# A two-layer transformer kernel on one core: the second layer's routing and its experts' weights moved into the first layer's expert loop

## The chip, the core and the metric

The kernel is one program on one core of a Trainium2 chip. The metric is the device time of one execution in microseconds (us), lower is better. TensorE (PE in the rows) multiplies matrices, VectorE (DVE) and ScalarE (ACT) work on tiles, GpSimd (POOL) does elementwise work and issues indirect DMAs, SyncE (SP) issues most other DMAs. Each engine runs its own instruction list in order; semaphores tie them together.

## The reference

1,024 tokens of 256 features go through two layers, each of a mixing part and a mixture of experts, all in float32:

```python
# layer 0
x = x + ga * attention(ln(x) * (1 + ca) + sa)            # 16 heads, causal
h = ln(x) * (1 + cb) + sb
x = x + gb * (shared_expert(h) + 64 small experts, top 6 of 64 by sigmoid, capacity 128)
# layer 1
h = ln(x) * (1 + ca) + sa
state_t = state_{t-1} * A + B h_t;  y = C state + h * D   # a scan over all tokens
x = x + ga * (ln(h + y) * w + b)
h = ln(x) * (1 + cb) + sb
x = x + gb * (8 experts of hidden size 512, top 2 of 8 by softmax, weights renormalised)
```

## The kernel before

**First expert layer (units).** It is computed densely: two halves of 512 tokens, each 17 hidden tiles (the shared expert and 16 tiles of four experts). So there are 34 units (`UNITS`), numbered u = 0 to 33; 0 to 16 are the first half's, 17 to 33 the second half's. A unit is `up(u)` on TensorE (two products of 12 matmuls), `gate_half` and `gated_high` on ScalarE, `gate(u)` and `gated_low(u)` on VectorE, and `down(u)` on TensorE, which accumulates in the bank pair `SUMS[h]`, (0,1) or (6,7). TensorE's list is `up(u)`, extras of unit u, `down(u - 2)`. Every float32 product is three matmuls of a high and a low part; SyncE loads each unit's weights (`load_weights`, seven buffers `w_raw`), GpSimd scales and splits them (`scale_down`, `weights_low`). The routing weights of a unit are a row block of `combine`, spread over partitions by `load_combine` into one of four buffers `wbc`; `gate` waits for it.

**Second layer's first half in the units.** When the first half's sums are complete (unit 16), its layer 1 work is threaded through units 18 to 33 by `if u == ...` lines on all engines: layer statistics, `both_rows(xn_h, 0, 0)` (eight transposes), `state_in` (matmuls), `scan` (DVE), `state_out`, `transpose_state`, `state_stats`, `state_weighted`, `state_added`, statistics again, `normalise_rows(4)` and `store_rows(0)` on ScalarE, `both_rows(xn_r, 0, 0)` at unit 32 and `router` at unit 33.

**Between the layers.** After the units VectorE does `route(0)` (softmax and top 2), TensorE counts pairs (`count_pairs(0)`, small matmuls with ones), VectorE makes eight full blocks of 128 pairs from the first half's tokens (`early_blocks`, `pair_places`, `pair_map`, `owners`), TensorE maps slots to tokens (`map_slots(0)`) and `slots(0)` writes the token indices. GpSimd then gathers the tokens' rows (`gather`). Beside this the second half's statistics run (`layer_out_stats(1)`; its root steps are interleaved with `early_blocks` by `input_norm`), ScalarE copies (`keep_rows(1)`) and normalises, TensorE transposes (`both_rows(xn_h, 0, 1)`), and `state_in(1)`, `map_weights(0)`, `state_out(1)` follow.

**Second expert layer (blocks).** 25 blocks b = 0 to 24 (`NB1`): 8 early ones (`NBE`) of the first half's tokens, 17 late ones. TensorE's list for a block is gate half of `half_up(b)`, `hidden(b-1)` (four transposes), `tokens(b+1)` (two transposes), value half of `half_up(b)`, `down1(b-1)`. The second half's remaining state work, its routing (`router`, `count_pairs(1)`, `map_slots(1)`, `map_weights(1)`) and its VectorE chain (`late_blocks` to `slots(1)`) are threaded through blocks 0 to 8. GpSimd's list is gather and scatter: block b's result is added to the sums in DRAM by `scatter(b)`; the gathers of late blocks are issued after `scatter(FIRST_LATE)`:

```python
            for b in range(NB1):
                scatter(b)
                if b == FIRST_LATE:
                    pool.wait_ge(slots_ready, 2)
                    pool.wait_ge(rows_stored, 32)
                    for c in range(NBE, b + NXG):
                        gather(c)
```

**Weights of the 8 experts.** `wgu` (1 MB for each expert) lies in SBUF over the first layer's unit buffers. One load is issued at unit 28, seven between the end of unit 30's `down` and the last one. TensorE waits for all 16 loads (`wgu` and `wdn`) ahead of block 0.

Of the kernel before, what the change touches and what calls it, by code (L numbers as in the profile page):

```python
# [13 lines left out]
P = 128  # L14
# [15 lines left out]
FIRST_LATE = 4  # L30
MAP_AT = (128, 256)
WEIGHTS_AT = (320, 352)
TOKENS1, HIDDEN1, DOWN1, ROUTE1, GATE1, VALUE1 = 0, 1, 2, 3, 4, 5
# [153 lines left out]
def program(nc, x_d, w_attn_d, w_out_d, qk_scale_d, gate0_d, ffn0_d, c_d, wmod_d, const_d,  # L187
# [9 lines left out]
    with ctx:  # L197
# [47 lines left out]
        sq = weights("sq", [P, HPG * HD])  # L245
        sqk = weights("sqk", [P, HD])
        (const,) = stage(("const", [P, 4 * P + 1], F32))
        qT_hi, qT_lo = [], []
        for c in range(2):
            qT_hi.append(weights(f"qT_hi{c}", [P, HPG, 512], F32R))  # L250
            qT_lo.append(weights(f"qT_lo{c}", [P, HPG, 512], F32R))
# [5 lines left out]
        weights("under_wo", [P, HPG, D])  # L257
        (v_hi, v_lo, prob, pT_hi, pT_lo, oT_hi, oT_lo, r_sb, o_f, mx, negb, rsum, rinv, rqs, gabs) = stage(
# [29 lines left out]
        w_sp, wbc, fa, _, _, _, fc, hid_hi, hid_lo = stage(  # L288
            ("w_sp", [P, NW, 2, 6 * P], F32R), ("wbc", [P, NC0, 512], F32), ("fa", [P, 2, 512], F32),
            ("beside_expert", [P, 2 * 256], F32), ("last_expert", [P, 8 * 256], F32), ("beside_fa", [P, 2, 512], F32),  # L290
            ("fc", [P, 2, 512], F32), ("hid_hi", [P, 2, 512], F32R), ("hid_lo", [P, 2, 512], F32R))
        (w_raw,) = stage(("w_raw", [P, NW, 2, 6 * P], F32))
        (wgu, chosen, placed, at_pair, fill, fill_key, picked, fill_top, taken,
         ends, count_i, pos_i, in_block, block_at, block_end, owner, code, token_f, empty, token_i, pair_i, owner_i,
         wpair, wslot, spare_row, fa1, hid1, slot_hot, block_hot, block_eq,
         pw_top, pw_rest, block_w) = stage(
            ("wgu", [P, E1, KC * 2 * H1], F32),
# [9 lines left out]
            ("slot_hot", [P, PAIRS, SLOTS1], BF16), ("block_hot", [P, PAIRS, 2 * NBL], BF16),  # L307
            ("block_eq", [P, PAIRS, NBL], F32), ("pw_top", [P, NT, TOPK1], BF16), ("pw_rest", [P, 2, NT, TOPK1], F32),
            ("block_w", [P, PAIRS, 3, NBL], BF16))
        keep("under_layers", [P, 88 * 256])  # L310
# [5 lines left out]
        hs = keep("hs", [P, T])  # L316
        zT = keep("zT", [P, KC, 512])
# [5 lines left out]
        x_b = keep("x_b", [P, NT, D])  # L323
        wmod1 = [wmod1_t[:, kc, :] for kc in range(KC)]
# [32 lines left out]
        yo_out = [sem(f"yo_out{b}") for b in range(NYO)]  # L357
        x_final, x_in_sums, weights_spread, weights_mapped = [sem(n) for n in (
# [17 lines left out]
        norm_step = sem("norm_step")  # L376
# [29 lines left out]
        def _(sp):  # L406
# [21 lines left out]
            def load_gate_up(e):  # L428
                sp.dma_start(wgu[:, e, :], gate_up_d[:, e, :]).then_inc(w1_loaded, 16)
# [26 lines left out]
            for u in range(1, 4):  # L456
                load_combine(u)
# [39 lines left out]
        def _(pool):  # L497
# [81 lines left out]
            for u in range(3, UNITS):  # L579
                weights_low(u)  # L580
                if u + 2 < UNITS:
                    scale_down(u + 2)
                if u == 25:
                    shifted_rows(0)
# [41 lines left out]
        def _(act):  # L626
# [200 lines left out]

            for u in range(UNITS):
# [25 lines left out]
                if u == 20:  # L854
                    act.wait_ge(x_kept, 2)
                    normalise_rows(3, tiles_of(0))
                if u == 22:
# [3 lines left out]
                if u == 31:  # L861
                    normalise_rows(4, tiles_of(0), last=True)
                if u == 32:
                    store_rows(0, 16)
                    act.wait_ge(z_ready, 2)
                    for kc in range(KC):
                        modulate(3, 1, 4, kc, SUMS[0] + kc)
                gated_high(u)
# [1289 lines left out]
```

## Time and profile before

| | |
|---|---|
| device time, three runs | 861.97, 862.66, 857.64 us (median 861.97) |
| profiled execution, its own device time | 857.57 us |
| its span, first to last instruction | 855.7 us |
| TensorE busy | 788.4 us (92%) |
| VectorE, ScalarE, GpSimd busy | 539.8, 459.6, 259.2 us |
| mean granted TensorE clock | 0.979 of full speed |
| units 18 to 33 with their last downs | about 594 to 672.3 us of the span |
| last down to block 0's first matmul | 672.3 to 691.5 us |
| blocks | 691.5 to 843.7 us, out copy 849.6 us |

Stages are given in us from the span's start. The last column pair of a windows row is DMA activity; the number ahead of it is the granted TensorE clock (1.00 is 2.4 GHz, 0.50 is 1.2 GHz).

### The profile page before, as it was taken

To read this page: it belongs to the slowest core of one execution; us is meant where nothing else is said; L and a number is where in the kernel's file an instruction comes from. 1 tells how busy PE (TensorE), PEld (TensorE's weight loads), DVE (VectorE), ACT (ScalarE), POOL (GpSimd) and SP (SyncE) were. 2 spreads that over 40 slices of the span, in tenths; PEclk is the share of its full clock that TensorE was granted. 3 is DMA by queue.
4 is the path that set the end of the run, shared out by engine and by line. 5 is a ranking of instruction groups with operands and counts; after the bars stand their busy time and mean duration, and the time that the engine had idled before them with its cause. 6 is when DMAs were issued, how large, how long until landed. Compare 5 with 4: busy or idle time off the path is not lost.

```text
span 855.7 us, 13741 instructions
## 1 busy us (share of the span) xinstructions
PE 788.4 (92%) x4674; PEld 642.5 (75%) x4674; DVE 539.8 (63%) x1321; ACT 459.6 (54%) x993; POOL 259.2 (30%) x185
## 2 busy tenths in 40 slices
PE   6887999989999989999899989999998589999994
PEld 5765888877788877888778778888887546666662
DVE  6567768677668667586786865685687776411211
ACT  3555766757648567467584825755544334233230
POOL 1004301017010061010150124666663033444432
PEclk9898999999999999999999999999999899999997
DMA  7010000010000100000010005565665822332322
GB/s 270 1 38 1 1 1 1 1 62 2 1 2 2 38 26 1 1 1 1 26 59 1 20 31 176 178 193 168 186 198 172 336 81 57 55 50 39 49 31 67
DMA packets 23459, 56.14 MB, mean 66 GB/s; under 512 B 2736, under 2 KB 10032, under 8 KB 22224
## 3 DMA queue, kind: packets, MB, share of 16 engines
q1 hardware_dynamic: 15792, 45.83, 16.2%
q0 software_dynamic: 4800, 6.56, 4.8%
q10 hardware_dynamic: 2800, 2.88, 1.0%
q8 instruction: 39, 0.64, 0.3%
q14 instruction: 28, 0.23, 0.1%
HBM read 48.97 MB, written 7.34 MB: 66 GB/s over the span
## 4 chain that ended last, share of the span: by engine, by line
PE 75%; DVE 11%; DMA 6%; ACT 3%; issue 3%; SPq 0%; POOLq 0%; DVEq 0%; ACTq 0%
PE ps L1632 16%; PE ps L1633 15%; PE ps L1634 15%; PE ps L2027 10%; PE ps L1737 6%; PE ps L2045 5%; DMA wbc<-combine 4%; DVE mx L1066 2%; DVE pT_lo L1080 1%; PE ps L1879 1%; PE ps L2037 1%; PE ps L1866 1%; DMA combine<-wT 1%; DMA wqkv_raw<-in_w_attn 1%; DVE o_f L1168 1%
## 5 line engine op out<-in xcount | busy, mean ns | idle before, releaser
L735 ACT ACTIVATE prob<-ps,negb,rqs 128x128 f32<-128x128 f32 (+7 forms) x128 | 106.7, 834 | 70.4 <-DVE negb L1071 69.0
L513 POOL TENSOR_TENSOR oT_lo<-o_f,oT_hi 128x512 fp32r<-128x512 f32 x32 | 41.6, 1300 | 301.4 <-ACT oT_hi L814 301.4
L724 ACT ACTIVATE pT_hi<-ps 128x512 fp32r<-128x512 f32 (+1 forms) x192 | 88.8, 491 | 63.3 <-PE ps L1737 57.7
L1066 DVE TENSOR_REDUCE mx<-ps 128x1 f32<-128x128 f32 (+7 forms) x128 | 96.5, 754 | 25.1 <-PE ps L1729 24.1
L1080 DVE TENSOR_TENSOR pT_lo<-ps,pT_hi 128x512 fp32r<-128x512 f32 (+1 forms) x192 | 99.9, 548 | 2.5 <-ACT pT_hi L724 2.4
L2027 PE MATMUL ps<-wgu,xgT 128*128 x200 | 94.2, 594 | 1.0 <-ACT xgT L888 1.0
L1737 PE MATMUL ps<-ident,prob 128*128 128x128 f32 x576 | 86.4, 276 | 0.9 <-DVE qT_lo L1102 0.6
L1632 PE MATMUL ps<-pT_hi,v_hi 128*128 128x512 f32 x192 | 73.6, 383 | 12.7 <-DVE pT_lo L1080 12.7
L1632 PE MATMUL ps<-kT_hi,qT_hi 128*128 128x512 f32 (+1 forms) x192 | 70.3, 366 | 5.6 <-ACT prob L735 3.9
L539 POOL TENSOR_TENSOR w_sp<-w_raw,w_sp 128x768 fp32r<-128x768 f32 x34 | 64.8, 1905 | 33.1 <-ACT w_sp L709 33.1
L1634 PE MATMUL ps<-kT_hi,qT_lo 128*128 128x512 f32 (+1 forms) x192 | 66.9, 348 | 0.0
L1633 PE MATMUL ps<-kT_lo,qT_hi 128*128 128x512 f32 (+1 forms) x192 | 66.8, 348 | 0.0
L1634 PE MATMUL ps<-pT_hi,v_lo 128*128 128x512 f32 x192 | 66.8, 348 | 0.0
L1633 PE MATMUL ps<-pT_lo,v_hi 128*128 128x512 f32 x192 | 66.6, 347 | 0.0
L602 POOL DMA_INDIRECT sums<-yo,pair_i x25 | 39.5, 1582 | 88.7 <-DVE yo L1571 72.0
L905 ACT ACTIVATE fa<-ps 128x512 f32<-128x512 f32 x25 | 14.9, 598 | 92.8 <-PE ps L2027 92.8
L1737 PEld LDWEIGHTS ps<-ident,prob 128*128 128x128 f32 x576 | 61.9, 142 | 2.9 <-DVE v_lo L1089 0.9
L1564 DVE TENSOR_TENSOR hid<-fa,ps 128x512 f32<-128x512 f32 x25 | 17.2, 687 | 70.9 <-PE ps L2027 65.3
L826 ACT ACTIVATE hid_hi<-fc 128x512 fp32r<-128x512 f32 x34 | 21.4, 631 | 65.3 <-DVE fc L1250 54.7
L2027 PEld LDWEIGHTS ps<-wgu,xgT 128*128 128x128 f32 x200 | 35.8, 190 | 26.7 <-issue 25.6
L1632 PE MATMUL ps<-hT_hi,w_sp 128*128 128x512 f32 x136 | 54.8, 403 | 0.3 <-issue 0.3
L1634 PE MATMUL ps<-hT_hi,w_sp 128*128 128x512 f32 x136 | 54.3, 400 | 0.0
(296 smaller groups left out, 2051.1 us busy)
## 6 DMA issues: line engine op xcount, KB each, us to landing
w_raw<-in_ffn SPq DMA_DIRECT2D x34, 384.0 KB, 6.8
wbc<-combine SPq DMA_DIRECT2D x32, 256.0 KB
wgu<-in_gate_up SPq DMA_DIRECT2D x8, 1024.0 KB, 8.9
wdn<-in_down SPq DMA_DIRECT2D x8, 512.0 KB, 10.2
wqkv_raw<-in_w_attn SPq DMA_DIRECT2D x4, 768.0 KB, 4.3
wo_raw<-in_w_out SPq DMA_DIRECT2D x4, 512.0 KB, 3.3
wmod_t<-in_wmod SPq DMA_DIRECT2D x1, 1536.0 KB, 13.9
x<-in_x ACTq DMA_DIRECT2D x2, 512.0 KB, 6.9
```

The costliest lines, as they stand in the source:

```text
L513: nc.gpsimd.tensor_tensor(oT_lo[:, m % HPG, :], o_f[:], oT_hi[:, m % HPG, :], ALU.subtract).then_inc(oT_lo_done, 1)
L539: nc.gpsimd.tensor_tensor(w_sp[:, b, 1, :], w_raw[:, b, 1, :], w_sp[:, b, 0, :], ALU.subtract).then_inc(w_ready, 1)
L724: nc.scalar.activation(pT_hi[:, unit % NUNITS, 0:nb, qi * P:(qi + 1) * P], ps[:, ROTATING[place % 3], 0:nb * P].rearrange("p (j t) -> p j ...
L735: nc.scalar.activation(prob[:, n % 3, 0:w], ps[:, pair:pair + 2, :].rearrange("p b k -> p (b k)")[:, 0:w], ACT.Exp, bias=negb[:, n % 2:n % ...
L1066: nc.vector.reduce_max(mx[:, i:i + 1], ps[:, pair:pair + 2, :].rearrange("p b k -> p (b k)")[:, 0:w], AX.X).then_inc(row_max, 1)
L1080: nc.vector.tensor_tensor(pT_lo[dst], ps[:, ROTATING[place % 3], 0:nb * P].rearrange("p (j t) -> p j t", j=nb), pT_hi[dst], ALU.subtract). ...
L1632: nc.tensor.matmul(out, w_hi_, m_hi, start=start, stop=False, skip_group_check=True)
L1633: nc.tensor.matmul(out, w_hi_, m_lo, start=False, stop=False, skip_group_check=True)
L1634: return nc.tensor.matmul(out, w_lo_, m_hi, start=False, stop=stop, skip_group_check=True)
L1737: ins = nc.tensor.transpose(ps[:, ROTATING[place % 3], j * P:(j + 1) * P], prob[:, k % 3, (j0 + j) * P:(j0 + j + 1) * P], ident[:])
L2027: ins = nc.tensor.matmul(ps[:, bank, :], xgT[:, b % 2, kc, :], wgu[:, bass.ds(e, 1), c:c + H1].rearrange("p a c -> p (a c)"), start=(kc == ...
L2045: ins = nc.tensor.matmul(ps[:, DOWN1, 0:D], hidT[:, b % 2, c, :], wdn[:, bass.ds(e, 1), c, :].rearrange("p a d -> p (a d)"), start=(c == 0 ...
```

## The change

It moves work between the three stages and reorders it.

- The first half's layer 1 chain runs two to four units earlier (statistics wholly at unit 18, transposes and modulate at 20, `state_in` 21, `state_out` 22, `transpose_state` 23, VectorE's steps packed in units 21 to 26, last transposes at 28, `router` at 29).
- `both_rows(…)` and `count_pairs(0)` in the units stand behind `down(u - 2)` instead of ahead of it.
- `route(0)`, the new `pair_weights(0)`, `early_blocks`, `pair_places`, `owners`, `pair_map` and `slots(0)` run in units 29 to 33; `count_pairs(0)` and `map_slots(0)` on TensorE in units 30 and 33. `chances(0)` (an Exp on ScalarE) is at unit 29.
- Banks: the routing of the two halves gets a bank each (1 and 3), so `count_pairs(1)` counts all eight tiles, not four.
- `load_combine` is issued one unit sooner. Weights of experts 0 and 1 are loaded at units 8 and 11, those of 3, 4, 5, 2, 6 as unit buffers come free, and expert 7's after the last `down`, under a semaphore of its own that TensorE waits for at block 4. SBUF tiles change places for this.
- Behind the last `down` TensorE does only `tokens(0)` and `both_rows(xn_h, 0, 1)` before block 0. `state_in(1)` and `map_weights(0)` come behind block 0's gate half, `state_out(1)` behind its value half, `transpose_state(1)` in block 1.
- In the blocks, `both_rows(xn_r, 4, 1)` and `router` move from block 3 to 4, `count_pairs(1)` from 4 to 5, `map_slots(1)` from 6 to 7, the VectorE chain to `slots(1)` with them by one block, and `FIRST_LATE` from 4 to 5.

```diff
-FIRST_LATE = 4
+FIRST_LATE = 5
+ROUTE1 = (1, 3)
...
-                if u % (1 + IT0):
-                    load_combine(u)
+                if u + 1 < UNITS and (u + 1) % (1 + IT0):
+                    load_combine(u + 1)
...
-                if u == 28:
-                    load_gate_up(7)
-
-            for e in range(3):
-                sp.wait_ge(down_done, UNITS - 4 + e)
-                load_gate_up(e)
+                if u in (8, 11):
+                    load_gate_up((u - 8) // 3)
+
+            sp.wait_ge(down_done, 29)
+            load_gate_up(3)
+            sp.wait_ge(down_done, 31)
+            load_gate_up(4)
+            sp.wait_ge(down_done, 32)
+            load_gate_up(5)
             sp.wait_ge(weighted, UNITS)
-            load_gate_up(5)
+            load_gate_up(2)
+            sp.wait_ge(down_done, 33)
             load_gate_up(6)
             sp.wait_ge(down_done, UNITS)
-            load_gate_up(3)
-            load_gate_up(4)
+            load_gate_up(7, w1_last)
...
# VectorE, in the loop over units
                 if u == 18:
                     layer_out_stats(0)
-                if u == 19:
                     variances(tiles_of(0))
                     root_steps(tiles_of(0))
                     shifts(tiles_of(0))
...
+                if u == 24:
+                    variances(tiles_of(0))
+                    root_steps(tiles_of(0))
+                    state_weighted(0)
+                if u == 25:
+                    state_added(0)
+                    link(stats(xt, tiles_of(0)))
                 if u == 26:
                     variances(tiles_of(0))
                     root_steps(tiles_of(0))
+                    shifts(tiles_of(0))
+                if u == 29:
+                    route_shift(0, SUMS[0])
+                    route(0)
+                if u == 30:
+                    pair_weights(0)
+                    early_blocks()
+                if u == 31:
+                    pair_places(HT)
+                    owners(NBE, 0)
+                if u == 32:
+                    pair_map(HT, NBE)
                 if u == UNITS - 1:
-                    route_shift(0, SUMS[0])
+                    slots(0, NBE, 0)
...
# TensorE, in the loop over units
+                if u == 29:
+                    pe.wait_ge(h_full, 12)
+                    router(wgate1, E1, SUMS[0], 0)
+                if u == UNITS - 1:
+                    map_slots(0, HT, NBE)
+                if u >= 2:
+                    down(u - 2)
+                if u == 30:
+                    count_pairs(0)
+                if u == 28:
+                    pe.wait_ge(rows_normed, 16)
+                    both_rows(xn_r, 0, 0)
+                if u == 20:
                     pe.wait_ge(rows_normed, 12)
                     pe.wait_ge(x_kept, 2)
                     both_rows(xn_h, 0, 0)
...
# TensorE, blocks
+            tokens(0)
+            pe.wait_ge(rows_normed, 18)
+            pe.wait_ge(ln_normed, NT + 2)
+            pe.wait_ge(x_kept, 4)
+            both_rows(xn_h, 0, 1)
             pe.wait_ge(owners_ready, 1)
-            pe.wait_ge(w1_loaded, 16 * 2 * E1)
-            tokens(0)
+            pe.wait_ge(w1_loaded, 16 * (2 * E1 - 1))
...
+                    if b == NBE - TB1:
+                        pe.wait_ge(w1_last, 16)
-                    if b == 6:
+                    if b == 7:
                         map_slots(1, NT, NBL)
-                    if b == 8:
-                        map_weights(1, NT, NBL)
                     half_up(b, e, 0, GATE1, gate_done)
                 if b == 0:
-                    transpose_state(1)
+                    state_in(1)
+                    map_weights(0, HT, NBE)
                 if b > 0:
                     hidden(b - 1)
                 if b + 1 < NB1:
                     tokens(b + 1)
...
+                if b == 0:
+                    state_out(1)
+                if b == 8:
+                    map_weights(1, NT, NBL)
```

## Rows read from the trace of the kernel before

**Rows 1.** Windows by stage: span; busy us (count) of PE, PEld, DVE, ACT, POOL; clock; DMA share; GB/s.
```profile
594.00:672.30 78.30, 74.94 (x434) 63.91 (x432) 54.10 (x118) 36.81 (x60) 37.65 (x27) 1.00 0.63 199
672.30:691.50 19.20, 8.48 (x49) 4.61 (x48) 16.39 (x87) 4.65 (x9) 5.89 (x5) 0.73 0.75 281
691.50:840.60 149.10, 149.09 (x637) 94.53 (x638) 52.73 (x161) 49.92 (x105) 57.63 (x45) 1.00 0.28 48
```
**Rows 2.** Waits of PE, 594 to 672.5 us: total us, times, longest.
```profile
PE ps L1646 <- ACT xn_r L677: 2.7, 1, 2.7
PE ps L1632 <- DVE hid_lo L1255: 0.6, 1, 0.6
```
**Rows 3.** Timeline of SP, two consecutive units: start us, us.
```profile
638.23 0.33 SPq L426 DMA_DIRECT2D w_raw<-in_ffn  x1
642.45 0.32 SPq L426 DMA_DIRECT2D w_raw<-in_ffn  x1
```
**Rows 4.** Timeline of PE between the layers: start us, us.
```profile
672.04 0.28 PE L1634 MATMUL ps<-w_sp,hid_lo 128*128 128x256 f32 x1
...
680.02 1.97 PE L1646 MATMUL ps<-ident,xn_h 128*128 128x128 f32 x8 [5.48 <-ACT xn_h L677]
...
691.51 1.98 PE L2027 MATMUL ps<-wgu,xgT 128*128 x4 [0.98 <-ACT xgT L888]
```
**Rows 5.** Timelines of DVE and ACT: the second half's statistics.
```profile
674.50 1.42 DVE L955 BATCH_NORM_STATS2 stat<-ps 128x6 f32<-128x256 f32 x4
...
678.88 1.09 ACT L677 ACTIVATE xn_h<-x,shift,rs_y 128x256 f32<-128x256 f32 x2 [1.84 <-DVE shift L975]
```
**Rows 6.** Critical chain, variances to shift of the first half: start us, us.
```profile
654.60 0.29 DVE mv L960 x4
656.70 1.72 DVE shift L975
```
**Rows 7.** Critical chain: moved TensorE groups where they run at full clock.
```profile
615.59 1.72 PE ps L1907 x4
...
741.34 0.42 PE ps L2001 x16
```
**Rows 8.** Windows of 2 us between the layers, columns as in group 1.
```profile
674.00:676.00 2.00, 0.51 (x14) 0.41 (x14) 1.86 (x8) 0.04 (x1) 0.00 (x0) 1.00 1.00 414
676.00:678.00 2.00, 0.00 (x0) 0.00 (x0) 1.97 (x19) 1.04 (x2) 0.00 (x0) 0.52 0.99 418
686.00:688.00 2.00, 1.11 (x10) 0.27 (x8) 1.66 (x5) 0.00 (x0) 1.42 (x2) 0.92 0.30 84
```
**Rows 9.** The tile wgu: time from issue to landing of its eight loads.
```profile
DMA to landing us min/median/max: 4.7/8.9/12.0
```
**Rows 10.** Timelines of PE, DVE and POOL, blocks 6 and 7.
```profile
729.05 0.56 PE L1991 MATMUL ps<-block_hot,slot_hot 128*128 128x34 bf16 x16
731.69 0.38 PE L2020 MATMUL ps<-ident,xg 128*128 128x128 f32 x2
...
737.51 0.38 PE L2020 MATMUL ps<-ident,xg 128*128 128x128 f32 x2
...
730.51 0.18 DVE L1529 TENSOR_SCALAR token_i<-token_f 128x17 int32<-128x17 int32 x1
...
730.25 1.55 POOL L602 DMA_INDIRECT sums<-yo,pair_i  x1 [3.54 <-DVE yo L1571]
732.11 1.01 POOL L589 DMA_INDIRECT xg<-rows,token_i  x1 [0.30 <-issue]
```
**Rows 11.** The tile xg: gathers over the whole kernel, then those of 680 to 700 us.
```profile
DMA to landing us min/median/max: 2.6/2.8/5.4
...
DMA to landing us min/median/max: 2.6/2.7/3.1
```
**Rows 12.** Timeline of DVE: unit 18's combine row arrives; a vector step of a unit.
```profile
595.43 0.69 DVE L1250 TENSOR_TENSOR fc<-ps,wbc 128x512 f32<-128x512 f32 x1 [2.32 <-DMA wbc<-combine]
...
646.74 0.69 DVE L1247 TENSOR_TENSOR ps<-fa,ps 128x512 f32<-128x512 f32 x1
```

More of the change, by code:

```diff
@@ L455, in _ @@
                 load_weights(u)
-            for u in range(1, 4):
+            for u in range(1, 5):
                 load_combine(u)
@@ L897, in hidden_in @@
                                      ACT.Copy).then_inc(hidT_ready, 1)
+            act.wait_ge(logits_done, 3)
             tokens_in(0)
+            for kc in range(KC):
+                modulate(4, 1, 0, kc, SUMS[1] + kc)
             for b in range(NB1 + 1):
@@ L1929, in both_rows, with count_pairs, map_slots, map_weights @@
                     transpose_rows(rows, t0, kc, SUMS[h] + kc)
+            def count_pairs(h):
+                pe.wait_ge(chosen_ready, h + 1)
+                bank = ROUTE1[h]
+                last = 4 * h + 3
+                for t in range(last + 1):
+                    for q in range(t + 1):
+                        nc.tensor.matmul(ps[:, bank, t * E1:(t + 1) * E1], (before_b if q == t else ones_b)[:],
+                                         sel_b[:, q, 0:E1], start=(q == 0), stop=(q == t), skip_group_check=True)
+                for q in range(last + 1):
+                    ins = nc.tensor.matmul(ps[:, bank, (NT + h) * E1:(NT + h + 1) * E1], ones_b[:], sel_b[:, q, 0:E1],
+                                           start=(q == 0), stop=(q == last), skip_group_check=True)
+                ins.then_inc(counted1, 1)
+            def map_slots(i, nt, nb):
+                pe.wait_ge(map_ready, i + 1)
+                hits = ps[:, ROUTE1[i], MAP_AT[i]:MAP_AT[i] + 2 * nb].rearrange("p (a n) -> p a n", a=2)
+                np_ = TOPK1 * nt
+                for j in range(np_):
+                    ins = nc.tensor.matmul(hits, slot_hot[:, j, :],
+                                           block_hot[:, j, :].rearrange("p (a n) -> p a n", a=2)[:, :, 0:nb],
+                                           start=(j == 0),
+                                           stop=(j == np_ - 1), skip_group_check=True)
+                ins.then_inc(mapped, 1)
+            def map_weights(i, nt, nb):
+                pe.wait_ge(weights_spread, i + 1)
+                sums = ps[:, ROUTE1[i], WEIGHTS_AT[i]:WEIGHTS_AT[i] + 3 * nb].rearrange("p (a n) -> p a n", a=3)
+                for j in range(TOPK1 * nt):
+                    ins = nc.tensor.matmul(sums, slot_hot[:, j, :], block_w[:, j, :, 0:nb], start=(j == 0),
+                                           stop=(j == TOPK1 * nt - 1), skip_group_check=True)
+                ins.then_inc(weights_mapped, 1)
             for u in range(UNITS + 2):
@@ L1974, in count_pairs @@
-            def count_pairs(h):
-                pe.wait_ge(chosen_ready, h + 1)
-                for t in tiles_of(h):
-                    for q in range(t + 1):
-                        nc.tensor.matmul(ps[:, ROUTE1, t * E1:(t + 1) * E1], (before_b if q == t else ones_b)[:],
-                                         sel_b[:, q, 0:E1], start=(q == 0), stop=(q == t), skip_group_check=True)
-                last = 4 * h + 3
-                for q in range(last + 1):
-                    ins = nc.tensor.matmul(ps[:, ROUTE1, (NT + h) * E1:(NT + h + 1) * E1], ones_b[:], sel_b[:, q, 0:E1],
-                                           start=(q == 0), stop=(q == last), skip_group_check=True)
-                ins.then_inc(counted1, 1)
@@ L1997, in map_weights @@
-            def map_weights(i, nt, nb):
-                pe.wait_ge(weights_spread, i + 1)
-                sums = ps[:, ROUTE1, WEIGHTS_AT[i]:WEIGHTS_AT[i] + 3 * nb].rearrange("p (a n) -> p a n", a=3)
-                for j in range(TOPK1 * nt):
-                    ins = nc.tensor.matmul(sums, slot_hot[:, j, :], block_w[:, j, :, 0:nb], start=(j == 0),
-                                           stop=(j == TOPK1 * nt - 1), skip_group_check=True)
-                ins.then_inc(weights_mapped, 1)
@@ L2005, in _ @@
-            count_pairs(0)
-            pe.wait_ge(rows_normed, 18)
-            pe.wait_ge(ln_normed, NT + 2)
-            pe.wait_ge(x_kept, 4)
-            both_rows(xn_h, 0, 1)
-            map_slots(0, HT, NBE)
-            state_in(1)
-            map_weights(0, HT, NBE)
-            state_out(1)
             def tokens(b):
```

337 lines of the change are left out of this document (141 added, 196 removed).

## The prediction, as it was put on record

> **What bounds the kernel now.** I read the windows by stage first, then TensorE's waits and timeline, then the chain. TensorE is busy for 149.09 of the 149.10 us of the blocks and for 74.94 of 78.30 us of units 19 to 33 [rows 1]: both loops run at the pace of TensorE. A unit takes 4.22 us, the distance of two loads that a finished `down` releases [rows 3]. Idle TensorE time in that stage is 2.7 us before the transposes at unit 32, which wait for ScalarE's rows, and 0.6 us before a `down` that waits for VectorE [rows 2]; the restarts behind them and slack between groups are about 1.0 us more, by the count of units and groups in the stage. Between the layers, from the last `down`'s end at 672.3 to block 0's first matmul at 691.5, TensorE is busy for 8.48 of 19.2 us while VectorE is busy for 16.39 [rows 1, 4]: the routing chain stands there, at a clock that falls to one half [rows 8]. So what can be won lies in 4.3 us of the units and 19.2 us between the layers; the blocks can only get longer.
>
> **The units.** Moved in: `count_pairs(0)` and `map_slots(0)`, 14 and 8 matmuls of a few columns; the 16 of `map_slots(1)` take 0.56 us [rows 10], so 0.5 and 0.4 us: +0.9 us. The other groups only change place within the stage. Gone if all is in time: the 4.3 us. What is late next is VectorE. A unit costs it three steps of 0.69 us [rows 12], 2.1 of 4.22 us; a low part may come some 8.4 us behind its `up` before TensorE waits, since two units of TensorE's work lie between. Unit 18 gets 1.42 us of statistics [rows 5] and the 2.1 us from variances to shift, which can be drawn out by up to 1.6 us (the shift itself took 1.72 us, where each of the ten steps takes about 0.2 [rows 6]). Carried forward from the combine row that lands at 595.4 [rows 12], unchanged since it waits for the same store: shift at 600 to 601.4, ScalarE's four rows (twice the 1.09 us of two [rows 5]) by 602.1 to 603.6, while TensorE wants them at 602.5 for the transposes at unit 20. A stall of 1.0 us. `load_combine` one unit sooner takes away VectorE's waits for rows, which TensorE felt only as the 0.6 us; at unit 17 it puts unit 21's weights behind a combine load that waits for its store, and what GpSimd then is late I count within the same 1.0. Unit 24 adds 3.7 us, unit 25 3.1, unit 26 2.1; carried forward in the same way, unit 26's low part and ScalarE's rows come 0 to 1.3 us late at unit 28: 0.5 us. Routing in units 29 to 32 adds some 10 to 14 linked steps each, at 0.2 us a step 2 to 3 us against the 2.1 free in a unit; the slack takes it up. In unit 33 `slots(0)`, seven steps, stands ahead of the low part: `down(33)` waits 0.8 us. Sum: -4.3 + 0.9 + 1.0 + 0.5 + 0.8 = -1.1, I take -1.0; the ends are -3.4 (no stall) and +2 (each chain drawn out once more). Experts 0 and 1 at units 8 and 11 add 2 MB where TensorE's weights are loaded units ahead: nothing, and if that cover were gone, one load's 2.6 us. The two table loads around `chances(0)` fall in ScalarE, busy for under half of the stage [rows 1]: nothing.
>
> **Between the layers.** What stays behind the last `down`: statistics 1.42, variances to shift 2.1, then ScalarE's two rows 1.09 [rows 5, 6], with semaphores 5.0 us; then eight transposes, 1.97 us as now at half clock [rows 4]. Together 7.0 against 19.2 us: -12.2. The tokens of block 0 are gathered from about 668.6 on and land in 2.6 to 5.4 us [rows 11], before the transposes. In these rows the six first gathers took 2.6 to 3.1 us [rows 11] though weights were still coming in at the start. The Trainium skill, DMA: Bandwidth & Descriptors, Queues, rings and completion order, says that a DMA engine goes round its queues packet by packet; by that rule the gather passes the weights' queue, and were it not so it would land some 8 us later and the gain of this stage would shrink by about 5 us. The trace agrees as far as it goes, but has no gather in the middle of 4 MB.
>
> **Weights.** Expert 5, 2 and 6 are released at about 667.5 to 669 and are 3 MB. At the 414 to 418 GB/s of [rows 8] that is 7.5 us, 676 to 677 with start and end; the transposes end near 678.3. Covered by 1.3 us. The loads took 4.7 to 12.0 us each in such a queue [rows 9]; at the upper end the wait would cost 3 us.
>
> **Work moved into the blocks.** `state_in(1)`, `state_out(1)` and `map_weights(0)` leave a stretch where TensorE was idle anyway and stand now where it is the bound: 1.72 us each for the two groups of four matmuls of 512 columns and 0.42 us, at full clock [rows 7], and ten more small matmuls in `count_pairs(1)`, 0.3 us: +4.1. The clock: before, TensorE stopped at 672.3, was at half by 676 and back at full about 6.3 us after the transposes began at 680.0 [rows 4, 8]. Now it stops for 5 us, so I expect the fall again, and the return some 6 us after the transposes start: block 0's gate half, as many columns as `state_in(1)`, at 1.2 GHz: twice 1.72 in place of 1.98 us [rows 4, 7], and 0.45 us of `state_in(1)`: +1.9. It could be 0 (no fall; the transposes would then be 1.0 us cheaper too). `down1(2)` waits about 0.3 us for `expert_out(1)`, which now stands behind the statistics of the new rows.
>
> **The late gathers.** Everything up to `slots(1)` moves one block back, but block 8's tokens are still wanted in block 7. Before: mapping at 729.05, indices at 730.69, scatter of block 4 from 730.25, first late gather at 732.11, landing 2.8 us later at about 734.9, and `tokens(8)` not before 737.51: 2.6 us in hand [rows 10, 11]. Now `tokens(8)` stands where `tokens(7)` stood, 2.6 us behind the mapping (731.69), and the rows land 5.9 us behind it: TensorE waits 3.2 us. On its queue behind that wait stand the value half and `down1(6)`. A block has nothing to hide it: +3.2, between 2.5 and 5.8 by the landing times of [rows 11].
>
> **Sum.** -1.0 - 12.2 + 4.1 + 1.9 + 0.3 + 3.2 = -3.7 us. The profiled execution took 857.57 us (855.7 us of span and 1.9 around it), so it would be 853.9. It lies at the foot of the three runs, 4.4 us under their median; on the median's footing I say 858. About 1% (8.6 us) is what a measurement here can tell from no change.
>
> **Rivals.**
> 1. More is won. The clock does not fall (-1.9 and -1.0) or the late gather is covered (-3.2), or both: -6.6, -6.9 or -9.8, so 848 to 851 on the profile's footing and 852 to 855 on the median's. For: the pause is 5 us against 7.7 before, and clock windows need not fall alike. Against: it had fallen after 3.7 us, and the gather's order is fixed in the list. Chance 0.30, both together 0.18.
> 2. The weights or the first tokens arrive late, since 4 MB, the gathers and the sums' store share the engines in 12 us: up to 3 to 5 us more, so -0.7 to +1.3, 861 to 863 on the median's footing. For: 1.3 us of cover only. Chance 0.15.
> 3. On the other side: VectorE becomes the bound of units 24 to 33. Its list holds about 25 linked small steps of routing ahead of `gated_low`, and each chain can be drawn out by 1.6 us as the shift was [rows 6]. Five chains drawn out give 8 us, 1.5 of them inside the slack; TensorE then waits before `down(29)` to `down(33)`: +6.5, so +2.8 over now, 865 on the median's footing. It decides when more than three chains are drawn out. For: GpSimd's splits run through unit 30. Against: VectorE is busy for 54.1 of 78.3 us [rows 1], and GpSimd stops there. Chance 0.10; about half of it or less passes +1%.
> 4. The change does not shorten the gap, because the second half's own chain was as long as the routing: out, its parts are 5.0 us [rows 5, 6]. Chance under 0.02.
>
> My forecast has 0.45. The range has to take in rival 1 and most of 2 and 3, and that the medians of three scatter by 5 us: 849 to 865. Faster by over 1% comes from rival 1 with both parts, and a little from a gap or a unit stage that is better than I think: 0.22. Slower by over 1% comes from rival 3 and its like: 0.08. Within 1%: 0.70.
>
> **What would show it.** The windows: last `down`'s end near 671.3, block 0's first matmul 7 us later, its duration 3.4 us (clock at half) or 1.7. TensorE's waits: about 3 us before the transposes of xg at block 7, and about 1 us before `both_rows` at unit 20. Blocks 1 to 24 otherwise at the same pace. I am wrong if the gap is over 10 us, if block 7 shows no wait, or if TensorE waits more than 4 us in the units.

## The result, and the profile after

| | before | after |
|---|---|---|
| device time, median of four runs | 862.03 us (857.64 to 862.66) | 877.12 us (876.91 to 877.19) |
| profiled execution: device time, span | 857.57, 855.7 us | 877.19, 875.4 us |
| mean granted TensorE clock | 0.979 | 0.971 |

After to before 1.0193, 95% interval 1.0162 to 1.0225: slower, by some 2%. I had forecast 858.0 us, 849 to 865. The profiled execution of before is as fast as the fastest of its four, so the two profiled ones lie 19.6 us apart where the medians lie 15.1.

I cut the span at three marks that every run here has: the start of `both_rows(xn_h, 0, 1)` at unit 5, the end of the last `down`, and block 0's first matmul. Up to the first mark the kernels are alike but for the first units.

| profiled execution, us | to unit 5 | unit 5 to last `down` | gap | block 0 to end | span |
|---|---|---|---|---|---|
| before | 533.2 | 139.1 | 19.2 | 164.2 | 855.7 |
| after | 535.5 | 153.6 | 9.9 | 176.4 | 875.4 |

"Gap" is the time between the last `down` and block 0. It did get shorter by 9.3 us and the blocks longer by 12.2; both have the predicted sign. The units, where I had a gain of 1.0, lost 14.5.

TensorE's waits of the changed kernel, units 5 to 29 (engine, tile, line, releaser: total us, times, longest):

```profile
PE ps L1618 <- POOL w_sp L546: 8.1, 8, 1.9
PE ps L1618 <- DVE hid_lo L1261: 1.2, 1, 1.2
PE ps L1754 <- ACT hT_h L662: 0.4, 1, 0.4
```

Up to the end of the units 1.3 us for `slot_hot` and 0.6 for a low part of `hid` are added, at unit 33. In [rows 2] no line on `w_sp` stands: TensorE now waits in `up` for GpSimd's low part of the weights, seven of the eight times between 563 and 616 us. One step back, GpSimd's timeline of the changed kernel, around the first of these stalls:

```profile
560.77 0.74 POOL L540 TENSOR_TENSOR w_raw<-w_raw,gates 128x256 f32<-128x256 f32 x1 [3.90 <-DMA w_raw<-in_ffn]
561.47 1.80 POOL L546 TENSOR_TENSOR w_sp<-w_raw,w_sp 128x768 fp32r<-128x768 f32 x1
565.72 0.89 POOL L540 TENSOR_TENSOR w_raw<-w_raw,gates 128x256 f32<-128x256 f32 x1 [2.45 <-DMA w_raw<-in_ffn]
```

GpSimd is early too; it waits for the load of `w_raw`. The chain of waits of the changed kernel names these loads (start us, us, what):

```profile
526.00 9.29 DMA w_raw<-in_ffn
...
552.95 12.70 DMA w_raw<-in_ffn
...
572.96 14.65 DMA w_raw<-in_ffn
...
601.62 11.04 DMA w_raw<-in_ffn
```

A load of 384 KB under way for 15 us: in the whole kernel they take 2.9, 8.5 and 14.8 us (least, median, most), where they took 2.9, 6.8 and 9.6. So look at the DMA engines, in windows where combine loads alone are moving: the first two of these three (the third is for the clock). The changed kernel (columns as in [rows 1]):

```profile
560.00:563.00 3.00, 1.40 (x12) 1.20 (x11) 1.18 (x2) 0.84 (x1) 2.23 (x2) 1.00 0.26 102
576.00:580.00 4.00, 3.07 (x42) 2.54 (x40) 2.84 (x3) 1.55 (x3) 2.29 (x2) 1.00 0.26 98
617.00:619.00 2.00, 2.00 (x6) 1.62 (x5) 0.82 (x1) 0.92 (x2) 2.00 (x2) 0.50 0.55 154
```

TensorE stands still for half of the first window, and the sixteen DMA engines are busy for 0.26 at 98 to 102 GB/s, where they can do 414 [rows 8]. The kernel before has the same figure, at the end of its units:

```profile
650.00:655.00 5.00, 5.00 (x33) 4.47 (x32) 4.37 (x13) 2.22 (x4) 2.68 (x3) 1.00 0.26 99
```

0.26 is, within a hundredth, four engines of sixteen. The load's source is four rows, each read 32 times, and four is the outermost dimension of its pattern. The Trainium skill, DMA: Bandwidth & Descriptors, in the section on why a DMA increments its semaphore by 16, has the rule: the number of engines is the largest one up to 16 that divides the slowest dimension that is not 1 of both patterns. The share agrees.

That gives the sum that I hadn't made. For each unit, one of the four engines moves 64 KB of a combine load, 24 KB of `w_raw` (384 KB over 16) and 10.7 KB of `wdn` (512 KB every third unit): 98.7 KB. At the rows' 25 KB/us (100 GB/s over four) this is, as an estimate, 3.9 of a unit's 4.22 us. Each early expert load adds 64 KB, 2.6 us, and 0.3 us is free in a unit: by this estimate two such loads three units apart make a queue that lasts to the end of the half (unit 17 needs no combine row). SyncE's list shows the same from the other side. I take it that an issue lasts longer when its queue has no room. SyncE, changed kernel:

```profile
557.59 2.00 SPq L445 DMA_DIRECT2D wbc<-combine  x1
559.63 3.29 SPq L433 DMA_DIRECT2D wgu<-in_gate_up  x1
562.97 0.59 SPq L430 DMA_DIRECT2D w_raw<-in_ffn  x1
563.66 0.57 SPq L445 DMA_DIRECT2D wbc<-combine  x1
564.27 3.65 SPq L474 DMA_DIRECT2D wdn<-in_down  x1
```

An issue of `w_raw` took some 0.33 us in [rows 3], those of `wgu` and `wdn` 0.33 to 0.49 us in the whole kernel before. The third window above shows a second price: TensorE had waited 1.8 us up to 615.7, and then ran at half clock until after 619.

TensorE in the gap, changed kernel, against [rows 4]:

```profile
692.67 0.69 PE L2001 MATMUL ps<-ident,xg 128*128 128x128 f32 x2 [3.60 <-DMA xg<-first_rows,token_i]
694.17 1.97 PE L1632 MATMUL ps<-ident,xn_h 128*128 128x128 f32 x8 [0.81 <-ACT xn_h L684]
699.00 3.78 PE L2008 MATMUL ps<-wgu,xgT 128*128 x4 [2.86 <-issue]
702.57 3.20 PE L1893 MATMUL ps<-hT_h,bT 128*128 128x512 f32 x4
```

and at block 7, against [rows 10]:

```profile
755.69 0.44 PE L2001 MATMUL ps<-ident,xg 128*128 128x128 f32 x2 [3.11 <-DMA xg<-rows,token_i]
755.96 3.17 PE L2008 MATMUL ps<-wgu,xgT 128*128 x4
758.92 2.34 PE L2026 MATMUL ps<-wdn,hidT 128*128 x8
```

The late gather costs 3.11 us where I had 3.2; that the clock then falls I had not counted. Four matmuls take 3.17 us there, and the next groups of the kind 1.88.

### The profile page after: what moved, and what is told of

Same layout as the page of the kernel before. It is cut to its first block, busy times and chain, and to the rows that moved or that the text cites. A ratio compares the mean times of both kernels' runs of the same rounds, so it can differ in the third digit from the quotient of the medians.

```text
span 875.4 us, 13755 instructions
## 1 busy us (share of the span) xinstructions
PE 801.0 (92%) x4684; PEld 649.3 (74%) x4684; DVE 544.4 (62%) x1321; ACT 461.3 (53%) x993; POOL 260.3 (30%) x185
## 4 chain that ended last, share of the span: by engine, by line
PE 70%; DVE 11%; DMA 9%; issue 4%; ACT 3%; POOL 1%; SPq 1%; POOLq 0%; DVEq 0%; ACTq 0%
PE ps L1618 14%; PE ps L1619 13%; PE ps L1620 13%; PE ps L2008 9%; PE ps L1723 6%; DMA w_raw<-in_ffn 5%; PE ps L2026 4%; DVE mx L1072 2%; DVE pT_lo L1086 1%; PE ps L1865 1%; DMA wgu<-in_gate_up 1%; PE ps L2018 1%; PE ps L1852 1%; PE ps L1641 1%; POOL w_sp L546 1%
## 5 line engine op out<-in xcount | busy, mean ns | idle before, releaser
L2008 PE MATMUL ps<-wgu,xgT 128*128 x200 | 97.4, 610 | 2.9 <-issue 2.9
L1618 PE MATMUL ps<-hT_hi,w_sp 128*128 128x512 f32 x136 | 57.0, 419 | 8.2 <-POOL w_sp L546 8.1
L2008 PEld LDWEIGHTS ps<-wgu,xgT 128*128 128x128 f32 x200 | 36.6, 194 | 29.6 <-issue 28.5
L1620 PE MATMUL ps<-hT_hi,w_sp 128*128 128x512 f32 x136 | 55.3, 407 | 0.0
L1619 PE MATMUL ps<-hT_lo,w_sp 128*128 128x512 f32 x136 | 55.1, 405 | 0.0
```

The costliest lines, as they stand in the source:

```text
L1618: nc.tensor.matmul(out, w_hi_, m_hi, start=start, stop=False, skip_group_check=True)
L1619: nc.tensor.matmul(out, w_hi_, m_lo, start=False, stop=False, skip_group_check=True)
L1620: return nc.tensor.matmul(out, w_lo_, m_hi, start=False, stop=stop, skip_group_check=True)
L2008: ins = nc.tensor.matmul(ps[:, bank, :], xgT[:, b % 2, kc, :], wgu[:, bass.ds(e, 1), c:c + H1].rearrange("p a c -> p (a c)"), start=(kc == ...
```

## The experiments

Theories: **A**, the combine loads keep four DMA engines nearly full and 2 MB more overflow them; **B**, the new place of `load_combine` in SyncE's list is the cause; **C**, VectorE's load is. Times are medians; the run of before on the same chips stood at 860.7 to 861.5.

**1. The order of the combine loads undone.**

```diff
-            for u in range(1, 5):
+            for u in range(1, 4):
                 load_combine(u)
...
-                if u + 1 < UNITS and (u + 1) % (1 + IT0):
-                    load_combine(u + 1)
+                if u % (1 + IT0):
+                    load_combine(u)
```

> Of the changed kernel one part is undone: load_combine is issued in its old order again (units 1 to 3 ahead of the loop, load_combine(u) instead of load_combine(u + 1) in it). Theory A (the two early expert loads are what is late: combine loads keep four of the sixteen DMA engines nearly full, at a DMA share of 0.25 to 0.27, and 2 MB more overflow them): GpSimd's waits for w_raw stay near 55 us, TensorE's waits for w_sp stay at 6 to 8 us, the time stays within 1.5 us of the changed kernel's. Theory B (the order is the cause: unit 17 puts unit 21's weights behind a combine load that waits for its store, and the combine load stands ahead of the weights' load): GpSimd's waits fall back to about 26 us, TensorE's waits for w_sp disappear, the kernel is 6 to 9 us faster than the changed one.

874.6 us (1.016 of before, 1.013 to 1.019), 2.5 us under the changed kernel: more than A's 1.5, far from B's 6 to 9. In the profiled executions the stages from unit 5 on gained nothing (340.3 us against 339.9; units 152.2 against 153.6). Some details speak for B: the waits for `w_sp` are gone but for 0.3 us, and GpSimd's for `w_raw`, from 520 to 675 us, fell from 45.2 to 33.1 us (26.1 before). But in their place TensorE waits for VectorE (from 520 us on), and VectorE for combine rows, 29.4 us where the changed kernel has 19.1:

```profile
PE ps L1618 <- DVE hid_lo L1261: 8.5, 7, 3.7
```

I read it so: weights and combine rows share the four engines, and the order only decides which of them is late. B is out as the cause of the lost time, and my expectation that the waits would stay where they were was wrong.

**2. Experts 0 and 1 loaded late.**

```diff
-                if u in (8, 11):
-                    load_gate_up((u - 8) // 3)
+                if u in (25, 28):
+                    load_gate_up((25, 28).index(u))
```

> Of the changed kernel the loads of experts 0 and 1 are issued at units 25 and 28 instead of 8 and 11. Theory A (2 MB overflow the four engines that the combine loads use): the stalls behind w_raw between units 11 and 24 disappear, 6.1 us of waits for w_sp between 560 and 610 among them, and come back in part behind unit 25, where ten units of queue are left, so 2 to 5 us of waits there; time 2 to 5 us under the changed kernel. Theory B (order of the combine load): the stalls stay where they are, between 560 and 616, and the time stays or rises by the 2 us of the later loads.

868.0 us (1.0087, 1.0062 to 1.0112), 9 us under the changed kernel where I had expected 2 to 5. Of 8.1 us of waits for `w_sp`, 0.4 stay. Units 145.1 us. The 2 MB at units 8 and 11 account for 8.5 of the 14.5 us that the units lost.

**3. Combine loads in four.**

```diff
-                sp.dma_start(wbc[:, k % NC0, :], rows0[i - 1][:, 512 * h:512 * h + 512].unsqueeze(1).to_broadcast(
-                    [EPT0, H0, 512])).then_inc(wbc_in[k % NC0], 16)
+                for j in range(EPT0):
+                    sp.dma_start(wbc[H0 * j:H0 * j + H0, k % NC0, :],
+                                 rows0[i - 1][j:j + 1, 512 * h:512 * h + 512].to_broadcast([H0, 512])
+                                 ).then_inc(wbc_in[k % NC0], 16)
```

VectorE waits for 64 in place of 16.

> Of the changed kernel each combine load is issued as four, one for each of the four expert rows, 32 partitions of 2 KB each. Theory A (the load's outermost dimension of 4 puts it on four of sixteen engines): each part is spread over all engines, the share in stretches that hold only combine loads rises from 0.25 to 0.27 toward 1 and they land sooner; GpSimd's waits for w_raw fall under 26 us, TensorE's waits for w_sp go, and with them the clock's fall at 617: 7 to 10 us faster than the changed kernel, about 868 to 870. Theory B (order): unit 17's weights are still blocked behind the wait for the store, 1.8 us of the waits and the fall of the clock near 616 stay, and the rest changes by under 2 us. Theory C (VectorE's load is the cause): no change beyond 1 us.

864.2 us (1.0039, 1.0021 to 1.0058): 13 us under the changed kernel, more than the 7 to 10 expected, with every load of it where it was. In the profiled executions 11.1 us of it lie behind the start of unit 5. In the one microsecond behind four such issues (587 to 588 us) the DMA share is 0.48, not the 1 that I had expected, but above 0.26. Time to landing of `w_raw` and SyncE's issues in this run:

```profile
DMA to landing us min/median/max: 2.9/3.9/6.8
```

```profile
588.20 1.76 SPq L446 DMA_DIRECT2D wbc<-combine  x4
590.00 0.42 SPq L476 DMA_DIRECT2D wdn<-in_down  x1
```

Waits for `w_sp` 0.3 us; From 520 us on VectorE waits 1.6 us for combine rows, where it waited 19.1 after the change and 29.6 before it. A holds; C does not explain the loss, for VectorE's work is the same here.

**4. Tokens of block 8 behind the value half.**

```diff
-FIRST_LATE = 5
+FIRST_LATE = 4
...
-                if b + 1 < NB1:
+                if b + 1 < NB1 and b + 1 != NBE:
                     tokens(b + 1)
...
                     half_up(b, e, 1, VALUE1, value_done)
+                if b + 1 == NBE:
+                    tokens(NBE)
```

> Of the changed kernel two lines: FIRST_LATE is 4 again, so the late gathers stand ahead of the scatter of block 5, and tokens(8) stands behind the value half of block 7 instead of ahead of it. By the prediction's step for the late gathers (TensorE waits 3.1 us with the value half queued behind it, and the clock falls behind the stop, about 1.7 us more in two groups at half clock): the wait shrinks from 3.1 to 0 to 0.5 us, the clock stays at 1.00 from 755 on, 3.5 to 4.8 us less than the changed kernel. Rival: the wait moves on to the gate half of block 8, which wants ScalarE's copy of the same rows, and only the scatter's 1.1 us are won.

871.3 us (1.0113, 1.0087 to 1.0140), 5.8 less; block 0 to end 171.1 us against 176.4. TensorE, at the same place:

```profile
752.89 0.44 PE L2001 MATMUL ps<-ident,xg 128*128 128x128 f32 x2 [0.23 <-DMA xg<-rows,token_i]
753.16 1.92 PE L2026 MATMUL ps<-wdn,hidT 128*128 x8
754.92 1.88 PE L2008 MATMUL ps<-wgu,xgT 128*128 x4
```

A 3.1 us stop in the blocks costs 5.3 us with the clock behind it, a little more than the 3.5 to 4.8 expected.

**5. The kernel before, combine loads in four.** Edit 3 on the kernel before.

> The kernel before with one edit: each combine load is issued as four, one for each expert row. Its TensorE waits for nothing that these loads hold up except 0.6 us for a low part and half a microsecond of the start of unit 18. Theory A (four engines nearly full, but not over in the kernel before): within 1.5 us of before, though VectorE's waits for wbc, 29.6 us now, shrink to under 15 and w_raw lands in 4 us at the median in place of 6.8. If instead the kernel before was already held up by these engines in a way that I don't see, it gains more than 3 us.

858.0 us (0.9959, 0.9939 to 0.9978): 2.8 us faster, between my two cases (from unit 5 on 321.3 us against 322.5 in the profiled executions). The 2.7 us wait for ScalarE's rows at unit 32 [rows 2] is gone with VectorE's waits for combine rows (29.6 to 2.2 us), so a good part of what the change set out to win in the units was this load too. Units 135.3 us, 3.8 less; the gap takes 2.3 back, at half clock until 690.

**6. The kernel before, combine loads in two.**

```diff
+                for j in range(0, EPT0, 2):
+                    sp.dma_start(wbc[H0 * j:H0 * j + 2 * H0, k % NC0, :],
+                                 rows0[i - 1][j:j + 2, 512 * h:512 * h + 512].unsqueeze(1).to_broadcast([2, H0, 512])
+                                 ).then_inc(wbc_in[k % NC0], 16)
```

> The kernel before with each combine load issued as two loads of two expert rows each (outermost dimension 2). If the outermost dimension sets how many DMA engines a load uses, each part runs on two engines: 256 KB then take 5.3 us or more in each unit of 4.2 us (2.67 us on four engines, twice that on two), the DMA share in stretches with combine loads alone is 0.13, TensorE waits for VectorE or GpSimd in most units, and the kernel is over 25 us slower than before. If the limit of 0.26 is the number of loads under way or the size of one load instead, two loads are as fast as one or faster and the time stays within 2 us.

935.3 us (1.0872, 1.0824 to 1.0921). Windows of this run with combine loads alone:

```profile
537.00:538.00 1.00, 1.00 (x10) 1.00 (x10) 0.00 (x0) 0.89 (x2) 0.86 (x1) 1.00 0.13 46
...
564.00:565.00 1.00, 1.00 (x10) 1.00 (x10) 0.00 (x0) 0.00 (x0) 0.85 (x1) 1.00 0.13 49
```

0.13 is two engines. If both halves of a load use the same two, 128 + 24 + 10.7 KB at 25 KB/us make 6.5 us for a unit; if they used different ones, each engine would have no more to move than before. From unit 5 to the last `down` it took 207.8 us, 68.7 more than before over 27 combine rows, so about 2.5 us more a unit: 6.7. That fits the same two. This is the rule's strongest test here, since the bytes and the work are the same.

**7. Both edits, 3 and 4.**

> The changed kernel with both edits, combine loads in four and the two lines for the late gathers (FIRST_LATE 4, tokens(8) behind the value half). The two stalls lie 80 us apart on different queues, so the gains add: 864.2 less the 5.8 us that the second edit gave alone, 858.4 us; if part of the 5.8 us was scatter between runs, 858.4 to 860.5. What stays against the prediction is then the gap between the layers at 10 us in place of 7 and 3 us of waits in the last units.

861.0 us (1.0009, 0.9990 to 1.0028), 0.5 us above the upper end of what I expected: as fast as before. To run 3 the second edit adds 3.2 us in the medians and 4.0 in the stages from unit 5 on, not 5.8: the blocks get 4.7 us shorter, the gap 0.7 longer.

**8. Expert 6 waited for at block 4.**

```diff
-            load_gate_up(6)
+            load_gate_up(6, w1_last)
...
-            pe.wait_ge(w1_loaded, 16 * (2 * E1 - 1))
+            pe.wait_ge(w1_loaded, 16 * (2 * E1 - 2))
...
-                        pe.wait_ge(w1_last, 16)
+                        pe.wait_ge(w1_last, 32)
```

> As the kernel with both edits, and expert 6's weights come under the later semaphore, so that TensorE waits for them at block 4 and not ahead of block 0 (for these inputs no earlier block has that expert). If the last 2.9 us ahead of block 0 are the weights (the chain runs through a load of 10.4 us that lands 1.1 us before the first matmul), one load of 1 MB less at 400 to 414 GB/s is 2.5 us: the gap is 7.5 us in place of 10.1, the kernel 2.5 us faster than the one with both edits. If it is GpSimd's gather or the clock that holds block 0, under 0.5 us.

856.1 us (0.9949, 0.9930 to 0.9969), 4.9 less than run 7, where 2.5 was expected. The gap is 6.9 us, the 7.0 of the prediction, so 3.7 of the 4.9 are there. The chain of run 3 (combine loads in four) shows what had stood there:

```profile
673.26 10.36 DMA wgu<-in_gate_up
683.62 1.15 issue
684.77 3.78 PE ps L2010 x4
```

"Issue" is here a wait for weights. The version rests on these inputs, in which no block before 4 has expert 6, and isn't one to keep.

**9. `map_slots(0)` behind `down(31)`,** by moving its two lines under those of `down(u - 2)`.

> The kernel with both edits (combine loads in four, tokens(8) behind the value half), and map_slots(0) stands behind down(31) instead of ahead of it. If its 2.2 us wait for slot_hot and the half clock behind it are what the last units cost beside the plan: down(31) covers 1.4 us of the wait, but slots(0) stands ahead of the low part of unit 33 on VectorE and now waits for the later mapping, so down(33) can come up to 2 us late: 0 to 2 us less than 861.0 us. If the clock's fall is what counts and it stays away: 2 to 3.5 us less.

857.4 us (0.9955, 0.9933 to 0.9977), 3.6 less than run 7 and, by the medians, faster than before; from unit 5 on the profiled executions show 1.6 us less than run 7, and 323.3 us against before's 322.5. The units are no shorter (143.5 us): 2.2 us of waits for `slot_hot` became 0.5, and those for low parts of `hid` rose from 2.1 to 3.1 us. There was no half clock to win back either: in run 7 it stands at 1.00 from 668 to 672 us, behind the same wait. The gap is what is shorter, 8.2 us against 10.6. The last load that block 0 waits for is issued at 672.10 and lands 10.35 us later, in run 7 at 672.41 and 11.61 us later. Why, I can't show; `down(31)`, which releases expert 5's load, no longer waits for the map.

**10. And `slots(0)` behind the low part of unit 33, `tokens(0)` behind `both_rows(xn_h, 0, 1)`.**

> As the one with map_slots(0) behind down(31), and slots(0) stands behind the low part of unit 33 on VectorE, and tokens(0) behind both_rows(xn_h, 0, 1) on TensorE. The wait for slot_hot and the half clock go from the last units (3 to 3.5 us), and the tokens come later, but block 0 still waits for its weights, which are released by the last downs: 3 us less than 861.0, so 858. If the weights are bound by DMA bandwidth from their release on, the last unit ends earlier but the releases too, so that the gap stays near 10 us. Rival: the gathers, now issued some 3 us later in the middle of the weights, land up to 8.2 us after their issue and hold block 0: no gain.

858.7 us (0.9964, 0.9939 to 0.9990), near the 858 expected, but not for the reason I gave. Units 143.1, gap 8.6: no better than run 9. TensorE's waits, 665 to 700 us:

```profile
PE ps L1634 <- ACT xn_h L686: 5.1, 1, 5.1
PE ps L1620 <- DVE hid_lo L1263: 1.3, 2, 1.0
PE ps L2010 <- ACT xgT L895: 1.0, 1, 1.0
```

Neither the gathers nor the weights are last here: the second half's own chain is, then the transposes, `tokens(0)` and ScalarE's copy in series.

**11. And expert 6 at block 4.**

> As the one before, and expert 6's weights are waited for at block 4. That edit gave 4.9 us to the kernel with both edits (861.0 to 856.1). If weights and last units are separate terms, 3 us more than that: 853. If the gathers become what is late, 856 or more and a wait of TensorE for xg of over 3 us ahead of block 0.

856.5 us (0.9952, 0.9929 to 0.9975), where I had 853: with weights no longer last, the series of run 10 sets the end (TensorE's three waits are the same), and the edit of run 8 is worth some 2 us, within the two intervals, and not 4.9.

**12. GpSimd's pass in two halves.**

```diff
-                nc.gpsimd.tensor_tensor(w_sp[:, b, 1, :], w_raw[:, b, 1, :], w_sp[:, b, 0, :],
+                nc.gpsimd.tensor_tensor(w_sp[:, b, 1, 0:3 * P], w_raw[:, b, 1, 0:3 * P], w_sp[:, b, 0, 0:3 * P],
+                                        ALU.subtract)
+                nc.gpsimd.tensor_tensor(w_sp[:, b, 1, 3 * P:], w_raw[:, b, 1, 3 * P:], w_sp[:, b, 0, 3 * P:],
                                         ALU.subtract).then_inc(w_ready, 1)
```

> The kernel with both edits, and GpSimd's pass over a unit's weights (1.82 us) is cut into two passes of half the columns, about 0.93 us each. In all ten cases so far a small VectorE step that took 1.3 to 1.8 us instead of 0.2 began less than 0.6 us behind the start of such a pass and ended with it. If the step is held until GpSimd's instruction ends, the longest small VectorE step in units 18 to 33 is now 1.0 us or less, the shift at unit 26 among them, and TensorE's wait for the low part behind it falls from 1.25 to about 0.4 us: 0.5 to 1.5 us less than 861.0. If the steps are drawn out for another reason (a semaphore, a queue), they stay at 1.7 us.

860.7 us (0.9987, 0.9967 to 1.0007): no measurable gain, but the mechanism is as expected. VectorE's shift in unit 26 without the edit (the run with combine loads in four), and GpSimd beside it:

```profile
638.75 1.70 DVE L983 SCALAR_TENSOR_TENSOR shift<-mv,rs_y 128x4 f32<-128x4 f32 x1
```

```profile
638.60 1.83 POOL L548 TENSOR_TENSOR w_sp<-w_raw,w_sp 128x768 fp32r<-128x768 f32 x1 [2.69 <-ACT w_sp L718]
```

and with it:

```profile
642.31 0.88 DVE L985 SCALAR_TENSOR_TENSOR shift<-mv,rs_y 128x4 f32<-128x4 f32 x1
...
682.00 2.35 DVE L1460 TENSOR_TENSOR pw_rest<-wpair,pw_top 128x8 f32<-128x8 f32 x1
```

```profile
642.16 1.02 POOL L548 TENSOR_TENSOR w_sp<-w_raw,w_sp 128x384 fp32r<-128x384 f32 x1 [2.70 <-ACT w_sp L720]
```

Both times the step ends with GpSimd's pass. The last step is beside GpSimd's `x_b` pass of 2.35 us, which was not cut, and keeps its length. The longest wait for a low part of `hid` fell to 0.6 us, from 1.2 in run 7.

Stages of the profiled executions, us:

| | median | to unit 5 | units | gap | blocks to end |
|---|---|---|---|---|---|
| 1 order back | 874.6 | 532.7 | 152.2 | 11.3 | 176.8 |
| 2 experts at 25, 28 | 868.0 | 533.2 | 145.1 | 10.0 | 176.0 |
| 3 in four | 864.2 | 531.9 | 143.0 | 9.9 | 175.9 |
| 4 tokens(8) | 871.3 | 535.6 | 152.2 | 10.7 | 171.1 |
| 5 before, in four | 858.0 | 534.3 | 135.3 | 21.5 | 164.5 |
| 7 both edits | 861.0 | 531.6 | 143.0 | 10.6 | 171.2 |
| 8 and expert 6 | 856.1 | 535.3 | 143.9 | 6.9 | 170.0 |
| 9 map behind down | 857.4 | 531.9 | 143.5 | 8.2 | 171.6 |
| 10 and slots, tokens | 858.7 | 535.0 | 143.1 | 8.6 | 171.4 |
| 11 and expert 6 | 856.5 | 531.4 | 142.2 | 8.5 | 170.8 |
| 12 halves | 860.7 | 535.0 | 142.4 | 10.1 | 170.4 |

The first column shows 4 us of scatter that no edit explains: it is in the stage all kernels share. Each row is one execution, so for differences of 2 to 4 us between runs the other columns belong beside the medians.

## Why the prediction was wrong

**The step that failed** is "Experts 0 and 1 at units 8 and 11 add 2 MB where TensorE's weights are loaded units ahead: nothing, and if that cover were gone, one load's 2.6 us". I looked at the mean DMA share of the stage, 0.63 [rows 1], and at loads issued three units ahead, and took both for room. The limit was four engines, by my estimate busy for 0.94 of their time, and the windows with 0.26 were in the profile. The price was no single 2.6 us either: with 0.3 us of slack in a unit a queue hardly drains, so each later load pays. Run 2 moves the loads and wins 9.1 us, run 3 gives the four engines room and wins 13.0, run 6 halves the engines and loses 74. With "`load_combine` one unit sooner takes away VectorE's waits" I also read those waits as an order's, when the load itself was slow: 19.1 of 29.6 us stayed. Undone, that part gives 2.5 us in the medians and nothing in the stages from unit 5 on. The 4.3 us that I had as gone were a little too many: [rows 1] has 3.4 us of idle TensorE (78.3 less 74.9), and run 5, where no wait is left, wins 3.8.

**VectorE in the units** (-1.0 in the sum). With the engines relieved, the changed units take 143.0 us and those of before, so relieved, 135.3: the moved work costs 7.7, of which `count_pairs` and `map_slots` are my 0.9. The rest is rival 3 in part: in run 3 TensorE waits 2.1 us for `slot_hot` at unit 33, 1.2 for a low part and 0.4 for `router`'s rows. Behind the wait at unit 33 the clock is also at half in run 3, 0.61 in the mean of 668 to 672; in run 7 it is not, and the units take as long. TensorE's waits with the 0.9 leave 2.8 us of the 7.7 in run 3, the clock's part among them, and 1.1 in run 7. I had placed a stall at `both_rows` of unit 20; there was none there.

**The gap**, 9.9 us and not 7.0. The parts were right, and run 8, with one load of weights less to wait for, shows 6.9. Rival 2 came true, at 2.9 us for weights. The loads of experts 5, 2 and 6 were issued at 685.4 to 686.8 us, ahead of the last `down`'s end by as much as I had said, but the last one landed at 697.9: 11 us in place of 7.5. From 688 to 700 us the DMA engines were nearly full throughout, but moved 359 GB/s in the mean and not 414, and the queue of the gathers took 12.0% of the engines' time. That explains a part; the rest stays open (expert 7's load, issued at 689.1, was under way too). The gathers did pass the weights' queue, as I had expected, and at a price: the six of 680 to 700 us landed 5.1 to 8.2 us behind their issue, where those of [rows 11] took 2.6 to 3.1.

**The blocks**, +12.2 for a predicted +9.5. The late gather was sized right (3.1 for 3.2), the moved work too: without the gather's stop it is 7.0 for a predicted 6.3 (run 7). Missing was the clock behind the stop, about 2 us (the 5.3 us of run 4 less the 3.1 of the wait).

**The sum.** Units 15.5 above the forecast, gap 2.9, blocks 2.7, the stage ahead 2.3 (scatter, as far as the runs show): 23.4 over 853.9, and the profiled execution took 877.2. The range left it out since its worst rival cost 6.5 us, and none of the four rivals was a shortage of DMA engines in the units.

## What to carry to other kernels

Ask of each DMA on how many engines it runs: a broadcast with a small outermost dimension fills few of them, and the mean share hides it (look at windows in which it is alone). Before bytes are added, sum the load of the busiest engine over one turn of the loop; beyond its pace each later transfer is late. Two versions to keep stand in the runs: the kernel before with its combine loads in four (0.9959), and the change with that, `tokens(8)` behind the value half and `map_slots(0)` behind `down(31)` (0.9955). Neither beats the other measurably, so the moved work itself won nothing that the runs can show: one edit on the kernel before gives as much.

## What the runs showed of the hardware that I had not expected

- Small VectorE steps are held by GpSimd's elementwise instructions. Between 592 and 700 us of all fourteen traces, 88 steps on tiles of at most 40 columns took over 0.5 us where such steps mostly take 0.16 to 0.2, and each of them ended within 0.05 us of the end of a GpSimd instruction. The longest took 0.74 us beside a 0.74 us pass, 1.78 beside one of 1.85, 2.35 beside one of 2.35, and 0.94 beside a pass cut to 1.02; a step that began in the middle of a pass was held for what was left of it. The Trainium skill, SBUF — State Buffer, Who interferes with whom, says that a VectorE instruction with two SBUF inputs contends with a GpSimd one that reads SBUF; the trace agrees for shift and pw_rest, which have two. Single-input steps were held as well (`rs_y` from `rs_in`, 1.73 us beside 1.81 in run 1). That I had named this "drawn out by up to 1.6 us" was right; that it is a matter of when GpSimd starts, I had not seen.
- TensorE's clock fell to one half behind stops of 1.8 us (unit 21), 2.1 us (unit 33 in run 3) and 3.1 us (block 7), while in the kernel before a stop of 2.7 us at unit 32 [rows 2], in the changed kernel one of 1.9 us ahead of 563.3 and in run 7 one of 2.2 us at unit 33 left it at full. I can't say from these rows what separates the cases.
- Seven of the ten issues of an expert's weights (`wgu`, `wdn`) on SyncE from 530 to 650 us took 2.2 to 3.9 us in the changed kernel, while the four engines were behind, and all ten took 0.42 with combine loads in four: long issues went with late loads.
